# The heads pass of a graph network kernel: sum and row of each head stacked for one product, eight row buffers, eight tiles unrolled

## The reference

```python
hh = h.reshape(n, H, D)                               # H = 12, D = 64
ft = jnp.einsum('nhd,ed->nhe', hh, W_fc)
a1 = jnp.einsum('nhd,hd->nh', ft, attn_l)
a2 = jnp.einsum('nhd,hd->nh', ft, attn_r)
e = jax.nn.leaky_relu(a1[src] + a2[dst], negative_slope=NEG_SLOPE)
m = jax.ops.segment_max(e, dst, num_segments=n)
ee = jnp.exp(e - m[dst])
denom = jax.ops.segment_sum(ee, dst, num_segments=n)
alpha = ee / denom[dst]
agg = jax.ops.segment_sum(alpha[:, :, None] * ft[src], dst, num_segments=n)
res = jnp.einsum('nhd,ed->nhe', hh, W_res)
return jax.nn.relu((res + agg).reshape(n, H * D))
```

## Time and profile before

| | |
|---|---|
| median of 3 runs | 3944.57 us |
| the profiled execution's own time | 3948.05 us |
| its span in the profile | 3946.3 us |
| PE busy | 3564.2 us (90%) |
| PE weight loads busy | 3357.4 us (85%) |
| DVE busy | 2495.6 us (63%) |
| ACT busy | 1368.4 us (35%) |
| POOL busy | 1093.1 us (28%) |
| heads pass, within the span | about 1782 to 2129 us |

### The profile page before, as it was taken

One profiled execution on the slowest core, in us unless ns is written; L12 is line 12 of the kernel. 1 busy time (PEld: TensorE's weight loads), 2 busy tenths in 40 slices (PEclk: granted clock), 3 DMA queues, 4 the chain that ended last, 5 costly groups with the idle time before them and its releaser, 6 DMA issues. The chain is left out here.

```text
span 3946.3 us, 64612 instructions
## 1 busy us (share of the span) xinstructions
PE 3564.2 (90%) x21099; PEld 3357.4 (85%) x21099; DVE 2495.6 (63%) x4989; ACT 1368.4 (35%) x1886; POOL 1093.1 (28%) x1515
## 2 busy tenths in 40 slices
PE   5899999999999788357996999997899998799999
PEld 5899999999999544137995899997799998799999
DVE  4977887148524488456996677776344443577777
ACT  2122232122222244214664344443333332344443
POOL 6530100314521100327885212211222111321121
PEclk8999999999999899778998999998899999899999
DMA  3576877657764488625664333333333333455554
GB/s 96 157 250 223 232 246 243 209 183 243 227 198 145 156 253 253 174 82 150 218 218 165 108 126 129 125 126 126 116 126 126 124 129 118 137 184 180 182 187 144
DMA packets 362673, 672.28 MB, mean 170 GB/s; under 512 B 99573, under 2 KB 192323, under 8 KB 362539
## 3 DMA queue, kind: packets, MB, share of 16 engines
q1 hardware_dynamic: 250698, 441.13, 36.7%
q10 hardware_dynamic: 67584, 155.63, 10.1%
q0 software_dynamic: 44256, 73.79, 6.7%
HBM read 429.75 MB, written 346.89 MB: 197 GB/s over the span
## 5 line engine op out<-in xcount | busy, mean ns | idle before, releaser
L709 DVE TENSOR_TENSOR fr_lo<-fr_turned_ps,fr_hi 128x768 fp32r<-128x768 f32 x158 | 150.3, 951 | 242.0 <-ACT fr_hi L1126 235.8
L2438 DVE SCALAR_TENSOR_TENSOR c3a_y<-c3a_prod,dinv,next_const 128x768 f32<-128x768 f32 x79 | 80.4, 1018 | 290.2 <-PE c3a_prod L2549 290.2
L1256 PE MATMUL fr_prod<-fr_w_hi,fr_hi 128*128 128x396 f32 x948 | 256.3, 351 | 0.0
L1256 PE MATMUL fr_prod<-fr_wu_hi,fr_hi 128*128 128x396 f32 x948 | 255.2, 350 | 0.3 <-issue 0.3
L2549 PE MATMUL c3b_prod<-next_w_hi,c3b_hi 128*128 128x384 f32 x948 | 249.7, 345 | 0.0
L2549 PE MATMUL c3a_prod<-next_w_hi,c3a_hi 128*128 128x384 f32 x948 | 249.4, 344 | 0.0
L2549 PE MATMUL cv_prod<-next_w_hi,cv_hi 128*128 128x384 f32 x948 | 249.4, 344 | 0.0
L1256 PE MATMUL fr_prod<-fr_wu_lo,fr_hi 128*128 128x396 f32 x948 | 248.4, 343 | 0.4 <-issue 0.4
L1256 PE MATMUL fr_prod<-fr_w_lo,fr_hi 128*128 128x396 f32 x948 | 248.5, 343 | 0.0
L1256 PE MATMUL fr_prod<-fr_w_hi,fr_lo 128*128 128x396 f32 x948 | 248.4, 343 | 0.0
L1256 PE MATMUL fr_prod<-fr_wu_hi,fr_lo 128*128 128x396 f32 x948 | 247.8, 342 | 0.0
(11 more groups left out here) (593 smaller groups left out, 9063.3 us busy)
## 6 DMA issues: line engine op xcount, KB each, us to landing
fr_ins<-in_x_dram SPq DMA_DIRECT2D x156, 384.0 KB
x<-fr_zrow SPq DMA_DIRECT2D x156, 384.0 KB
x<-up_x_o ACTq DMA_DIRECT2D x78, 396.5 KB
h<-fr_outs SPq DMA_DIRECT2D x78, 396.0 KB
u<-fr_outs SPq DMA_DIRECT2D x78, 396.0 KB
up_ut<-u SPq DMA_DIRECT2D x78, 396.0 KB
agg<-fr_zrow SPq DMA_DIRECT2D x78, 390.0 KB
hds_row<-x SPq DMA_DIRECT2D x78, 384.0 KB
```

What stands on the lines that cost most here:

```text
L709: v.tensor_tensor(lo[:, s2, :, :], turned_ps[:, 0:KC, :], hi[:, s2, :, :].bitcast(F32), ALU.subtract).then_inc(split_done, 1)
L1256: made = nc.tensor.matmul(prods[s2][:, bank, 0:c1 - c0], l[:, s2, s, :], w[:, s, c0:c1], start=(s == 0 and i == 0), stop=(s == KC - 1 and ...
L2438: v.scalar_tensor_tensor(y3, p3, g["dinv"][:, bass.ds(t, 1)], c3, ALU.mult, ALU.add).then_inc(prod_read, 1)
```

## The change

The two matrices now stand one below the other, W_fc on lanes 0 to 63 and W_res on lanes 64 to 127 of a 128 x 64 tile `w_st`. `x` has, for each head, 64 columns of the sum and beside them 64 of the row. The second half is a copy of the row by ScalarE, one tile ahead (`beside`). TensorE transposes the 128 columns of each head and multiplies once with `w_st`: 12 transposes, as before, and 12 products with 64 columns in place of 12 with 128. All transposes now wait for the add and for the copy. There are eight buffers for the rows, with SyncE up to eight tiles ahead; `more` and `x_o` keep four. The loop body of this pass has eight tiles; tiles 0 to 7 and 72 to 78 stand outside. The memset of the matrices is gone, and each is loaded once. The lines of the changed kernel differ: L2201 is the scale, L2230 the add, L2224 own weights, L2250, L2252, L2254 the three small ones, L2238 the former L2240, L2279 the new copy, L2285 the copy of the transposed tile, L2333 and L2342 transposes and products.

```diff
-def over_tiles(eng, step, drain=0):
+def over_tiles(eng, step, drain=0, unroll=UNROLL):
...
-    H, F = 12, D
+    H, F, WIDE = 12, D, 2 * UNROLL
...
-        row, more = sb("row", [P, UNROLL, D]), sb("more", [P, UNROLL, AGG_W])
+        row, more = sb("row", [P, WIDE, D]), sb("more", [P, UNROLL, AGG_W])
...
-        own_w, x, y = sb("own_w", [P, 2, H]), sb("x", [P, 2, D]), sb("y", [P, 2, D])
+        own_w, x, y = sb("own_w", [P, 2, H]), sb("x", [P, 2, H, 2, F // H]), sb("y", [P, 2, D])
...
-        w_st = sb("w_st", [P, 2, P])
+        w_st = sb("w_st", [P, F // H])
...
-            sp.wait_ge(w_zero, 1)
...
-                    for q in range(2):
-                        sp.dma_start(w_st[64 * q:64 * q + 64, k, 64 * q:64 * q + 64], w.rearrange("e d -> d e")).then_inc(w_in, 16)
+                    sp.dma_start(w_st[64 * k:64 * k + 64, :], w.rearrange("e d -> d e")).then_inc(w_in, 16)
...
-                if at_least(t, UNROLL):
-                    sp.wait_ge(prod_read, t - UNROLL + 1)
+                if at_least(t, WIDE):
+                    sp.wait_ge(prod_read, t - WIDE + 1)
                 sp.dma_start(row[0:rows_of(t), slot, :], tile_rows(x1, t)[:, 0:D]).then_inc(loaded[slot], 16)
...
-            nc.gpsimd.memset(w_st[:, :, :], 0.0).then_inc(w_zero, 1)
             nc.gpsimd.memset(more[:, :, :], 0.0).then_inc(cleared, 1)
...
-                nc.gpsimd.tensor_tensor(x[:, s2, :].rearrange("p (h f) -> p h f", h=H), row[:, slot, :].rearrange("p (h f) -> p h f", h=H),
+                nc.gpsimd.tensor_tensor(x[:, s2, :, 0, :], row[:, slot, :].rearrange("p (h f) -> p h f", h=H),
                                         own_w[:, s2, :].unsqueeze(2).to_broadcast([P, H, F // H]), ALU.mult).then_inc(scaled, 1)
...
-                v.scalar_tensor_tensor(x[:, s2, :], more[:, slot, 0:F], g["has_in"][:, bass.ds(t, 1)], x[:, s2, :],
-                                       ALU.mult, ALU.add).then_inc(built, 1)
+                v.scalar_tensor_tensor(x[:, s2, :, 0, :], more[:, slot % UNROLL, 0:F].rearrange("p (h f) -> p h f", h=H),
+                                       g["has_in"][:, bass.ds(t, 1)], x[:, s2, :, 0, :], ALU.mult, ALU.add).then_inc(built, 1)
...
+            def beside(t, slot, turn):
+
+                act.wait_ge(loaded[slot], turn * 16 + 16)
+                if at_least(t, 2):
+                    act.wait_ge(turned, t - 1)
+                nc.scalar.activation(x[:, slot % 2, :, 1, :], row[:, slot, :].rearrange("p (h f) -> p h f", h=H), ACT.Copy).then_inc(copied, 1)
...
-                pe.wait_ge(loaded[slot], turn * 16 + 16)
-                for s in range(KC):
-                    nc.tensor.transpose(turned_ps[:, KC + s, :], row[:, slot, s * P:(s + 1) * P], g["ident"][:, :])
+                pe.wait_ge(copied, t + 1)
                 pe.wait_ge(built, t + 1)
-                for s in range(KC):
-                    made = nc.tensor.transpose(turned_ps[:, s, :], x[:, slot % 2, s * P:(s + 1) * P], g["ident"][:, :])
+                for s in range(H):
+                    made = nc.tensor.transpose(turned_ps[:, s, :], x[:, slot % 2, s, :, :].rearrange("p k f -> p (k f)"), g["ident"][:, :])
...
-                for s in range(KC):
-                    o = prods[s2][:, s // 3, (s % 3) * P:(s % 3 + 1) * P]
-                    nc.tensor.matmul(o, hi[:, s2, s, :], w_st[:, 0, :], start=True, stop=False)
-                    made = nc.tensor.matmul(o, hi[:, s2, KC + s, :], w_st[:, 1, :], start=False, stop=True)
+                for s in range(H):
+                    made = nc.tensor.matmul(prods[s2][:, s // 6, (s % 6) * 64:(s % 6) * 64 + 64], hi[:, s2, s, :], w_st[:, :], start=True, stop=True)
```

More of the change, by code:

```diff
@@ L87, in at_least, with back @@
     return not isinstance(t, int) or t >= k
-def over_tiles(eng, step, drain=0):
-    for t in range(UNROLL):
+def over_tiles(eng, step, drain=0, unroll=UNROLL):
+    for t in range(unroll):
         step(t, t, 0)
-    with eng.Fori(1, NT // UNROLL) as i:
-        for j in range(UNROLL):
-            step(i * UNROLL + j, j, i)
-    for t in range(NT // UNROLL * UNROLL, NT + drain):
-        step(t, t % UNROLL, t // UNROLL)
-def back(t, slot, turn, lag):
-    return t - lag, (slot - lag) % UNROLL, turn + (slot - lag) // UNROLL
+    with eng.Fori(1, NT // unroll) as i:
+        for j in range(unroll):
+            step(i * unroll + j, j, i)
+    for t in range(NT // unroll * unroll, NT + drain):
+        step(t, t % unroll, t // unroll)
+def back(t, slot, turn, lag, unroll=UNROLL):
+    return t - lag, (slot - lag) % unroll, turn + (slot - lag) // unroll
 def live(t):
@@ L2155, in heads_pass @@
         prods = [ctx.enter_context(nc.psum_tensor(f"hds_prod{i}", [P, 2, 512], F32)) for i in range(2)]
-        loaded = [sem(f"loaded{j}") for j in range(UNROLL)]
+        loaded = [sem(f"loaded{j}") for j in range(WIDE)]
         more_in = [sem(f"more_in{j}") for j in range(UNROLL)]
         stored = [sem(f"stored{j}") for j in range(UNROLL)]
-        w_zero, w_in, cleared, indexed, owned, scaled, built = (sem("w_zero"), sem("w_in"), sem("cleared"), sem("indexed"),
+        w_in, cleared, indexed, owned, scaled, built = (sem("w_in"), sem("cleared"), sem("indexed"),
                                                                 sem("owned"), sem("scaled"), sem("built"))
+        copied = sem("copied")
         turned, hi_done, multiplied, prod_read = sem("turned"), sem("hi_done"), sem("multiplied"), sem("prod_read")
@@ L2215, in _ @@
             scale(0, 0, 0)
-            over_tiles(pool, step)
+            over_tiles(pool, step, 0, WIDE)
         @block.vector
@@ L2260, in step @@
                     add(t, slot, turn)
-                b = back(t, slot, turn, -1)
+                b = back(t, slot, turn, -1, WIDE)
                 if live(b[0]):
                     own(*b)
-                b = back(t, slot, turn, 3)
+                b = back(t, slot, turn, 3, WIDE)
                 if at_least(t, 3) and live(b[0]):
                     shift_of(*b)
-                b = back(t, slot, turn, 2)
+                b = back(t, slot, turn, 2, WIDE)
                 if at_least(t, 2) and live(b[0]):
@@ L2295, in store @@
                 act.wait_ge(polished, t + 1)
-                act.dma_start(tile_rows(x2, t), x_o[0:rows_of(t), slot, :]).then_inc(stored[slot], 16)
+                act.dma_start(tile_rows(x2, t), x_o[0:rows_of(t), slot % UNROLL, :]).then_inc(stored[slot % UNROLL], 16)
             def step(t, slot, turn):
+                b = back(t, slot, turn, -1, WIDE)
+                if live(b[0]):
+                    beside(*b)
                 if live(t):
                     high(t, slot, turn)
-                b = back(t, slot, turn, 2)
+                b = back(t, slot, turn, 2, WIDE)
                 if at_least(t, 2) and live(b[0]):
                     root_of(*b)
-                b = back(t, slot, turn, 3)
+                b = back(t, slot, turn, 3, WIDE)
                 if at_least(t, 3) and live(b[0]):
                     polish(*b)
-                b = back(t, slot, turn, 4)
+                b = back(t, slot, turn, 4, WIDE)
                 if at_least(t, 4) and live(b[0]):
                     store(*b)
-            over_tiles(act, step, 4)
+            beside(0, 0, 0)
+            over_tiles(act, step, 4, WIDE)
             for j in range(UNROLL):
@@ L2315, in _ @@
         def _(pe):
-            pe.wait_ge(w_in, 64)
+            pe.wait_ge(w_in, 32)
             def turn_over(t, slot, turn):
@@ L2342, in step @@
                     turn_over(t, slot, turn)
-                b = back(t, slot, turn, 1)
+                b = back(t, slot, turn, 1, WIDE)
                 if at_least(t, 1) and live(b[0]):
                     multiply(*b)
-            over_tiles(pe, step, 1)
+            over_tiles(pe, step, 1, WIDE)
 def conv_pass(nc, g, tag, table, out, res=None, last=False):
```

22 lines of the change are left out of this document (11 added, 11 removed).

## The result

| | us |
|---|---|
| before, median of 4 runs (3943.55 to 3948.07) | 3946.28 |
| after, median of 4 runs (4016.8 to 4021.5) | 4021.01 |
| ratio after to before, 95% interval | 1.0187 (1.0172 to 1.0202) |
| profiled execution of after: its time, its span, mean granted clock | 4021.03, 4019.2, 0.956 |

The change costs 75 us, 1.9%. The forecast was 4010 us, in a range of 3960 to 4040.

What follows compares the result with a forecast made beforehand. TensorE was taken as the bound, 3.99 us per tile, VectorE close at 3.80. Held tiles add 70.4 us from tile 4 to 78, the start gives -5.2: +65.2 on 3944.57 makes 4010 us, range 3960 to 4040.

Steps and rivals of the forecast that it cites:

- 1: TensorE products in the heads pass: 64 columns cost what 128 do, nothing saved, TensorE keeps 3.99 us per tile.
- 2: All 12 transposes wait for the add and the copy: +1.2 us once in the first tile, later nothing.
- 3: New ScalarE copy of 768 columns, 834 ns, issued for the next tile: cost 0, ScalarE at 3.5 us per tile.
- 4: Start of the pass: two weight loads for four and no memset wait bring the first scale 5.5 us earlier.
- 5: Eight row buffers: all 27 waits of the scale for rows go; the scale starts 1.25 us after the add.
- 6: Strided x for scale and add, and loop turns: taken as 0, at most 7 us and 2 us in all.
- 7: Small VectorE instruction held until the GpSimd scale ends: 5.03 us per tile in the loop, 4.82 outside it.
- 8: From tile 3, GpSimd is idle before each next own weights, so the early scale recurs in every tile; nothing ends it.
- rival C: The held state begins but breaks at loop turns or after a late gather, then begins again: 3975 us; chance 0.05.
- A: GpSimd's gather keeps the scale late, nothing is held, TensorE stays the bound: 3935 us; chance 0.12.
- B: As A, and products take half, so VectorE's 3.80 us per tile bounds: 3921 us; chance 0.05.
- D: TensorE, partly idle with less moving data, falls to 1.2 GHz and bounds at 7.3 us per tile: 4180 us; chance 0.04.

Runs made afterwards that it cites:

- e9: e3 with 128 moving columns in each product instead of 64, the weights read twice; 3939.47 us, ratio 0.9988 to before.
- e3: The changed kernel with the three small VectorE operations moved ahead of the next tile's own weights; 3935.60 us, ratio 0.9975 to before.
- e10: The changed kernel with 128 moving columns in each product instead of 64, the weights read twice; 4015.59 us, ratio 1.0186 to before.
- e2: The kernel before with only eight row buffers and eight tiles unrolled, old products, transposes and weight loads, no copy; 4022.05 us, ratio 1.0196.
- e6: e2 with the three small VectorE operations moved ahead of the next tile's own weights; 3943.45 us, ratio 0.9992 to before.
- e1: The changed kernel with each row load waiting, as before, for the product four tiles back; 3949.07 us, ratio 1.0003 to before.
- e4: The changed kernel with one added GpSimd wait: the scale waits for the last small operation of the tile four back; 3934.16 us, ratio 0.9970.
- e5: The changed kernel with two small VectorE operations rewritten to take one input tile and a scalar per lane; 3934.88 us, ratio 0.9976.
- e8: e3 with each head's product made as two of 32 columns instead of one of 64; 4490.81 us, ratio 1.1376 to before.

## Why the prediction was right

Direction, mechanism and place held. The tile of 5.03 us was a little small, and the loop turns, put at nothing, cost 4 us; together with the low clock and a slightly better start that makes the difference between +65 and +71.

1. *Products of 64 columns cost what 128 do: nothing saved.* Right: e9 against e3, 2.84 and 2.79 us for 24 records. By the gap in the Trainium skill's page "TensorE: Matmul & The Clock Gate", section "Back-to-back issue gap", they would have taken about 1.3 us, the estimate made ahead. The section gives that gap for isolated products and says that it counts too little at few columns, since it leaves out the weight loads; the measured 2.79 us agrees with that.
2. *Twelve transposes behind the add: 1.2 us once.* From the first scale to the add of tile 3 it is 15.3 us, before 14.6: 0.7 us more, by one trace each. Later they delay nothing that shows: where the small ones are held, e10 takes 375.9 us for the 74 tiles and e2, with the old transposes, 375.9 too; where nothing is held, 296.3 in e3 and 295.1 in e6. With late rows (e1) they may.
3. *The copy L2279 at 834 ns is hidden.* Its row after is 833 ns, and e3 runs at TensorE's pace with it.
4. *Two weight loads: the first scale 5.5 us earlier.* 5.8 measured, by the two traces, from the start of the pass; 5.7 by e6 and e3.
5. *Eight buffers: the waits for rows go, and the scale comes 1.25 us behind the add.* 1.28 within the loop. e2 has this part alone and all of the loss; e1 takes it alone away, and the loss is gone.
6. *Strided x and loop turns cost nothing.* Half right. The strided add has a mean of 998 ns, before 1010, and the scale 1471 and 1478. But a loop turn costs 0.5 us in the held state, 4 us in the eight turns, where the text allowed for at most 0.2 us each: one interval in eight is 5.55 us in place of 5.06, while the next two differ by +0.11 and -0.11.
7. *L2254 or L2256 is held, tile 5.03 us.* Shown by e3, e4 and e5, which remove the hold in three ways and land within 1.5 us of each other. The interval is 5.06 us (1.28 to the scale, 1.61 from there to L2238, 2.17 to the next add; forecast 1.25, 1.60, 2.18), and 5.12 on average with the loop turns. This is the term that was too small: 74 tiles take 377.1 us, forecast 370.1. Of the 7 us, 64 x 0.09 = 5.8 are the step from 5.03 to 5.12, 2 of them the tile and 4 the loop turns, and 1.2 the spells of low clock, which e10 is without.
8. *The state holds itself.* It begins in tile 3, as forecast, and never breaks: rival C is out. In e2 it begins one tile later and stays likewise. The prediction counted two tiles of before in which the scale held a small instruction; there is a third, in tile 75 (2103.84, above). It did not start the state either, since the next scale again waited for its row, and this hold, which begins ahead of the scale, is not one that the prediction's account explains. And GpSimd's 3.4 us of work per tile were too high a count, mostly because the add lengthened L83 in 50 tiles; after, it is 2.8 (27.80 us over 9.9 tiles). GpSimd is idle again before the next own weights either way, which is all that the argument needs.

The sum: forecast +70.4 - 5.2 = +65.2. Measured +77.4 in the 74 tiles and -6.0 up to tile 4 (28.8 us from the start of the pass to the add of tile 4, before 34.8), so +71.4. The profiled executions differ by 4021.03 - 3948.05 = 73.0; 1.95 us of that lies ahead of the pass.

The forecast of 4010 us lies 11 us under the median of 4021. Of these, 1.7 us are its basis: it started from 3944.57, the median of three runs, where the four runs have 3946.28.

Of the rivals, A described the versions that work: TensorE as the bound, 74 tiles at 3.99, 3935 us. e3, e4 and e5 measured 3934 to 3936. It failed here because GpSimd's queue does not keep the scale late by itself. B is out, since the products did not take half. D came true in small: TensorE's clock did fall with the narrow products, for a tile at a time; where it was down for most of the pass, in e8, it cost some 320 us of the 74 tiles, by the estimate above.

## What to carry to other kernels

A wait that costs nothing can be what keeps two engines out of each other's way. Before removing it, list what the freed instruction will start beside, and look in the trace for a tile where that already happens: here three tiles of 79 held a small instruction, and two of them showed the later state of nearly all. If a tiny instruction lasts as long as a large one on GpSimd and ends with it, either issue it ahead, let the large one wait, or write it with one input tile and a scalar per lane; each was worth 85 to 87 us here.

## What the runs showed of the hardware

- A VectorE instruction on one number per lane with two SBUF inputs, 0.16 us by itself, lasted 1.32 to 1.43 us in the kernel after where it started while a GpSimd product of 768 columns ran. In the form with one input tile it took 0.21 us at the same place. A VectorE instruction of 768 columns with one input from SBUF and one from the accumulators started inside the GpSimd product in e5 and kept its 0.96 us.
- It holds the other way too: a GpSimd addition on one number per lane, 0.19 us by itself, lasted 0.9 to 1.0 us when it started behind VectorE's add of 768 columns with two SBUF inputs, and ended with it.
- TensorE's products with 128 stationary rows and columns in float32 follow each other at 0.11 us per record, with 32, 64 or 128 moving columns, at the full granted clock, and at 0.21 us at the low level (1.2 GHz), with 32 columns as with 64: 10.29 us for 48 records in e8, 5.22 for 24 in this row of the kernel after.

```profile
1876.59 5.22 PE L2342 MATMUL hds_prod<-hds_w_st,hds_hi 128*128 128x64 f32 x24
```

- In the stretches of 50 us from 1900 to 2100 us the granted clock was under 1.00 only in kernels with narrow products. In the stretch from 1900 to 1950 us it was 1.00 in the kernel before, in e2 and in e10 (128 columns), 0.93 in the kernel after and 0.91 in e1 (64 columns), and in the middle of e8 (32 columns) 0.60, with TensorE busy all the time. But it was 1.00 in e3, e4 and e5 with 64 columns too, where TensorE hardly pauses. What decides it was not settled.
